# Where TensorE's operands lie in SBUF: moving them from 128 or 192 bytes past a 2048-byte multiple to the multiple itself, in a two-layer graph network kernel

## The reference

```python
# layer 0
deg = sum(adj, axis=-1, keepdims=True)
agg = einsum('bij,bjf->bif', adj, x) / maximum(deg, 1e-6)
x   = layernorm(x + relu(einsum('bnf,of->bno', concat([x, agg], 2), W)))
# layer 1
Ah  = adj + eye(N);  dh = rsqrt(sum(Ah, -1))
out = einsum('bnm,bmf,fc->bnc', dh[:, :, None] * Ah * dh[:, None, :], x, kernel) + bias
x   = layernorm(x + relu(out))
```

## The kernel before

| operand | columns | start of the tensor, mod 2048 | step between rows or blocks |
|---|---|---|---|
| `adj_hi`, `adj_lo`, moving | 512 | 128 | 2048 |
| `adj_hi`, `adj_lo`, stationary | 128 | 128 | 512 |
| `xt_*`, `g1_*`, `x1s_*`, stationary | 128 | 128 | 512 |
| `z_hi`, moving | 258 | 128 | 1032 |
| `z_lo`, moving | 256 | 192 | 1024 |
| `w_hi`, `w_lo`, moving | 512 | 192 | 2048 |
| `k_hi`, `k_lo`, moving | 256 | 192 | 1024 |

## Time and profile before

### The profile page before, as it was taken

The page is one execution under the profiler, slowest core; times in us unless marked ns, Lnnn a source line. Parts: engine busy times, 40 slices in busy tenths (PEclk is TensorE's granted clock), DMA queues, the critical chain, the costliest instruction groups (busy, mean ns, idle before and its releaser), DMA issues.

```text
span 513.6 us, 8698 instructions
## 1 busy us (share of the span) xinstructions
PE 495.7 (97%) x3072; PEld 446.8 (87%) x3072; DVE 388.7 (76%) x1020; ACT 243.9 (47%) x483; POOL 0.7 (0%) x6
## 2 busy tenths in 40 slices
PE   4999999999999999999999999999999999999992
PEld 3898889988899888998889988998889988899872
DVE  4788397984888857986679858798498974898556
ACT  5825437364283643645454553636437364263312
POOL 0000000000000000000000000000000000000000
PEclk9999999999999999999999999999999999999997
DMA  8934401634018140362305631064401614020002
GB/s 287 382 139 165 165 0 41 223 145 163 0 77 280 51 163 0 110 257 77 127 0 173 229 120 50 8 237 163 163 0 41 245 41 164 0 83 1 0 1 82
DMA packets 15978, 59.78 MB, mean 116 GB/s; under 512 B 1760, under 2 KB 1888, under 8 KB 15072
## 3 DMA queue, kind: packets, MB, share of 16 engines
q1 hardware_dynamic: 15968, 59.64, 32.8%
HBM read 51.25 MB, written 8.39 MB: 116 GB/s over the span
## 4 chain that ended last, share of the span: by engine, by line
PE 96%; DVE 2%; DMA 1%; ACT 0%; SPq 0%; issue 0%; ACTq 0%
PE ring_a L564 15%; PE ring_a L562 15%; PE ring_a L563 14%; PE ring_b L595 11%; PE ring_b L597 11%; PE ring_b L596 11%; PE ring_b L562 6%; PE ring_b L563 6%; PE ring_b L564 6%; DMA xt_raw<-xT 1%; DVE u L405 0%; DVE stats L414 0%; DVE x L409 0%; SPq L175 0%; DVE xt_lo L346 0%
## 5 line engine op out<-in xcount | busy, mean ns | idle before, releaser
L562 PE MATMUL ring_a<-z_hi,adj_hi 128*128 128x258 f32 x512 | 144.9, 283 | 0.0
L564 PE MATMUL ring_a<-z_hi,adj_lo 128*128 128x258 f32 x512 | 144.4, 282 | 0.0
L563 PE MATMUL ring_a<-z_lo,adj_hi 128*128 128x256 f32 x512 | 142.9, 279 | 0.0
L595 PE MATMUL ring_b<-adj_hi,x1s_hi 128*128 128x512 f32 x256 | 100.0, 391 | 0.0
L597 PE MATMUL ring_b<-adj_hi,x1s_lo 128*128 128x512 f32 x256 | 99.8, 390 | 0.0
L596 PE MATMUL ring_b<-adj_lo,x1s_hi 128*128 128x512 f32 x256 | 99.6, 389 | 0.0
L563 PEld LDWEIGHTS ring_a<-z_lo,adj_hi 128*128 128x128 f32 x512 | 97.3, 190 | 0.0
L564 PEld LDWEIGHTS ring_a<-z_hi,adj_lo 128*128 128x128 f32 x512 | 96.2, 188 | 0.0
L562 PEld LDWEIGHTS ring_a<-z_hi,adj_hi 128*128 128x128 f32 x512 | 95.9, 187 | 0.0
L346 DVE TENSOR_TENSOR adj_lo<-adj_raw,adj_hi 128x1024 fp32r<-128x1024 f32 x64 | 75.0, 1221 | 3.5 <-ACT adj_hi L223 2.8
L223 ACT ACTIVATE adj_hi<-adj_raw 128x1024 fp32r<-128x1024 f32 x64 | 62.8, 1056 | 0.0
(11 more groups left out here) (66 smaller groups left out, 685.1 us busy)
## 6 DMA issues: line engine op xcount, KB each, us to landing
adj_raw<-adjT SPq DMA_DIRECT2D x64, 512.0 KB, 6.1
x_sb<-x SPq DMA_DIRECT2D x16, 512.0 KB, 5.0
out<-x SPq DMA_DIRECT2D x16, 512.0 KB, 2.6
xt_raw<-xT SPq DMA_DIRECT2D x7, 1024.0 KB, 4.8
x<-w SPq DMA_DIRECT2D x2, 256.0 KB, 3.4
xt_raw<-xT SPq DMA_DIRECT2D x2, 256.0 KB, 4.6
xt_raw<-xT SPq DMA_DIRECT2D x1, 512.0 KB, 6.1
x<-k SPq DMA_DIRECT2D x1, 256.0 KB, 8.8
```

The lines of the kernel that those rows point to most:

```text
L562: nc.tensor.matmul(o, lhi, rhi, start=(first and i == 0), stop=False)
L563: nc.tensor.matmul(narrow, lhi, rlo, start=False, stop=False)
L564: last = nc.tensor.matmul(o, llo, rhi, start=False, stop=last_part)
L595: nc.tensor.matmul(ring_b[:, bank, :], lhi, ahi, start=(j == 0), stop=False)
```

## The change

Each operand of TensorE is placed at a multiple of 2048 bytes within a partition. For this `sb` takes an alignment, the small tensors are declared first, then the operands, then the rest. From 16,512 the small ones reach 18,336, so `adj_hi` starts at 18,432 = 9 x 2048, and every operand after it has a size that is a multiple of 2048. The row of `z_hi` grows from 258 to 320 elements, 1280 bytes, so that the tensor has 10,240 bytes; the matmul still reads 258 of them. The instructions, their order, the semaphores and the DMAs are the same.

```diff
+LINE = 2048
+ZROW = 320
...
-        def sb(name, shape, dt=F32):
-            return ctx.enter_context(nc.sbuf_tensor(name, shape, dt))
+        def sb(name, shape, dt=F32, align=32):
+            return ctx.enter_context(nc.sbuf_tensor(name, shape, dt, align_bytes=align))
...
+        a_hi = sb("adj_hi", [P, H * T * NH], F32R, LINE)
+        a_lo = sb("adj_lo", [P, H * T * NH], F32R, LINE)
+        w_hi = sb("w_hi", [P, FT, 2 * F], F32R, LINE)
+        w_lo = sb("w_lo", [P, FT, 2 * F], F32R, LINE)
+        k_hi = sb("k_hi", [P, FT, F], F32R, LINE)
+        k_lo = sb("k_lo", [P, FT, F], F32R, LINE)
+        z_lo = sb("z_lo", [P, T, F], F32R, LINE)
+        z_hi = sb("z_hi", [P, T, ZROW], F32R, LINE)
+        xt_hi = sb("xt_hi", [P, FT, N], F32R, LINE)
+        xt_lo = sb("xt_lo", [P, FT, N], F32R, LINE)
+        x1s_hi = sb("x1s_hi", [P, T, F], F32R, LINE)
+        x1s_lo = sb("x1s_lo", [P, T, F], F32R, LINE)
+        g1_hi = sb("g1_hi", [P, FT, NH], F32R, LINE)
+        g1_lo = sb("g1_lo", [P, FT, NH], F32R, LINE)
...
-                                     z_hi[:, j, :], z_lo[:, j, :])], j == 0, j == T - 1)
+                                     z_hi[:, j, 0:F + 2], z_lo[:, j, :])], j == 0, j == T - 1)
```

## The result

The changed kernel takes 514.53 us (median of 11 runs, 513.89 to 515.49) against 515.73 us for the kernel before on the same chip (11 runs). The ratio is 0.9979, with a 95% interval of 0.9971 to 0.9987: faster by 0.2%. The medians are 1.2 us apart where the forecast had a gain of 4.3 us and a time of 511.0 us. The profiled execution went from 513.6 to 512.4 us of span, but the spans of the changed kernel's eleven executions lie between 511.7 and 513.3 us.

A forecast was written before the change was run, and what follows sets the result against it. TensorE's step between matmul starts was taken to bound the kernel. Terms of 0.56 us a batch over eight batches, less 0.27 and plus 0.12 for project0, gave 4.3 us: 511.0 us, range 504 to 518.

The forecast's parts named there:

- The bound: Between 20 and 500 us TensorE waits for nobody; only the step between matmul starts can change, surplus 5.2 us a batch.
- project0 at propagate's pace: project0's w rows and weights at the same relative place take propagate's 226.7 ns a step, gaining 0.27 us a batch.
- The sign that was named for it: In project0, weight loads at 188 ns would show the forecast right; 193 was read before.
- Heads of propagate: Propagate's slow matmuls after project0 and project1 (12 at 230.0, 24 at 228.3 ns) speed up, gaining 0.08 us a batch.
- Propagate's steady step stays: Both propagate operands move together, so its 226.7 ns step was taken to gain nothing.
- Aggregate at project1's pace: Aggregate's step, 119.5 ns, falls by 1.1 ns toward project1's 117.9 plus 0.6, gaining 0.21 us a batch.
- project1 at nothing: project1's step of 117.9 ns was taken to gain nothing, on the ground that propagate's operands move together.
- The longer rows of z_hi: In aggregate, rows of 1280 bytes start every z row on a multiple of 256; taken to gain 0.21 us a batch.
- odd step: In aggregate, step 1 takes 0.37 us against step 0's 0.35; the odd step was called slow in all 64 tiles.
- Rival 1: Absolute place causes the whole surplus on every matmul: 474 us; chance 0.14 in full or in large part.
- Rival 2: Place doesn't reach TensorE's pace; stretches differ by order and shapes, time stays 515.3 us; chance 0.18.
- Rival 3: Moving stream and weight load collide at one phase; propagate's 96 matmuls lose 6.4 ns each, 520 us; chance 0.12.

The follow-up runs named there:

- the probe: Kernel body replaced by groups of matmuls, no layer computed; pairs give row, then weight offset in bytes past a multiple of 2048; 512 columns at (0, 0): 226.7 ns.
- the first probe: Kernel body replaced by groups of 64 equal matmuls, 19 pairs of row and weight offsets, 512 and 256 columns; (64, 0) with 256 columns: 113.3 ns.
- the second: Kernel body replaced by groups of 32 triples (hi, lo, hi rows), each behind 24 wide matmuls, weights at 0; 256 columns with rows at 64: 117.8 ns.

## Why the prediction was wrong

- **The bound.** Right. TensorE waits for nobody in the middle, and the time follows the sum of its steps: 8 x 0.13 us a batch is 1.0 us, and the span fell by 1.2. That the two come so close is in part chance: from the first aggregate's start to the last one's (seven batches) the gain is 0.88 us, the first aggregate starts 0.47 us earlier, and the rest takes 0.15 us longer. That first start lies anywhere from 20.16 to 21.35 us in the nine profiled kernels.
- **project0 at propagate's pace.** Right: 226.9 and 226.7 ns, against 226.7. The experiment that moves w alone shows that its relative place is the cause. The sign that was named for it, weight loads of 188 ns instead of 193, was misread: the 193 is a mean over all of project0's loads, those of graph 0 at the lower clock among them. In batch 1 they take 189 ns before and 188 after.
- **Heads of propagate.** Right for the first, 0.04 us. The head behind project1 gave 0.02 instead of 0.04 us; with k at 192 it goes whole (24 matmuls in 5.44 us).
- **Propagate's steady step stays.** Right, 226.7 ns, and with all operands at 128 too.
- **Aggregate at project1's pace, and project1 at nothing.** This is the step that failed. For the narrow matmuls of aggregate it took 117.9 ns, a step measured in project1, where the k rows lay 64 bytes past the weights' place (192 against 128), while the change put the z rows at the weights' place. And it costed project1 at nothing with a reason that speaks of propagate alone; k went from 64 bytes past the weights' place to that place. There the narrow step is 120.0 ns. Aggregate lost 0.10 us a batch where a gain of 0.21 was forecast, and project1 lost 0.10 where nothing was. Together that is 0.41 of the 0.44 us that the batch fell short, and 8 x 0.41 = 3.3 us stands against the 3.1 us between the forecast gain of 4.3 and the measured 1.2. The kernel with k and z at 64 confirms it: project1 is back at 117.9 ns and aggregate at 118.3. For aggregate the prediction's bounds, "nothing, or all 12.3 ns", had no slow side at all.
- **The longer rows of z_hi** were costed as a gain; by themselves they cost 0.21 us of aggregate in a batch. Without them the change would have gained 61.60 - 61.29 = 0.31 us a batch, near the 0.35 us that the forecast had without its term for `z_hi`. The prediction also read a slow "odd step" from the rows before. Only step 1 is that slow: step 5, also odd, takes 0.354 us in the mean of the 64 tiles, step 1 takes 0.366.
- **The rivals.** Rival 1 (absolute place, 474 us) is refuted by the result, with propagate at 226.7 ns on the multiple too, and by the kernel with everything at 128. The Trainium skill (TensorE: Matmul & The Clock Gate, Back-to-back issue gap) gives columns plus 2.5 ns; the probe has 2.7 ns in bfloat16, but 13.4 ns in float32r at the best place, so that rule doesn't carry to these matmuls. Rival 2 (no effect) fell with w's 64 bytes; the Trainium skill (SBUF — State Buffer, Who interferes with whom) has matmul and weight load on ports of their own with no waiting, and by that one would expect their relative place not to matter, while the probe has 226.7 ns at (0, 0), 227.2 at (128, 128) and 233.3 at (128, 0). Rival 3 (streams in each other's way at one phase) named the right kind of loss but the wrong matmuls: the wide ones gained, the narrow ones paid.

## What to carry to other kernels

Where TensorE runs without gaps, take the step from start to start, stretch by stretch and shape by shape, and don't lend one shape's best placement to another. For float32r operands here the place of the moving row relative to the weights, within 256 bytes, was worth about 1 to 3.5% of a step for wide matmuls (226.7 ns at the same place, 228.8 to 234.7 elsewhere). For narrow ones the same place takes 119.9 ns, the best of those tried 113.7 and the worst 129.7. A probe with the kernel's own pattern of matmuls agreed with the narrow steps of the kernel to 0.3 ns in all but one case, while for wide ones off the best place it was up to 4.5 ns short. The change's own idea gives 0.2%; with z at 32 and k at 112 the same instructions give 1.1%.

## What the hardware showed that I had not expected

- The step depends on the relative place within 256 bytes, not on crossing a multiple of 2048: rows at 0, 256, 512 and 1024 take 226.7 to 227.2 ns, at 8 or 32 bytes 233.4.
- One pair of places can have several paces: project0 with w at 64 takes 229.2 ns a step in its first stretch in the loop and 233.3 in the later ones, and (64, 0) with 256 columns took 113.3 ns in the first probe and 117.8 in the second, with another pattern of matmuls.
- Eight bytes can make 16 ns with 256 columns: 129.7 at 104 against 113.7 at 112.
- With rows at 0 a smaller weight load gives a longer step: 231.7 ns with 32 weight columns, 226.7 with 128. With rows at 128 it gives 230.8 against 233.1.
